# Two-bank row maxima on halves of the TensorE rows, in a transformer stack of two attentions and two feed-forwards

## The reference

```python
x = x + cross_attention(layernorm(x), ctx, mask, Wq, bq, Wk, bk, Wv, bv, Wo, bo)   # 16 heads of 16, 77 keys
x = x + mixture(layernorm(x), ...)            # 6 experts of 128, the top 2 of them weighted, gelu
x = x + shared_key_attention(layernorm(x), ctx, w_q, w_kv, w_concat)  # 16 query heads, one key/value head
x = x + fixed_point_ffn(layernorm(x), ...)    # 256 -> 1024 -> 256, rounded, piecewise-linear gelu
```

## Time and profile before

| | us |
|---|---|
| median of three runs | 789.1 (788.37 to 789.65) |
| the profiled execution's own time | 788.65 |
| its span | 786.4 |
| a block of the first attention (161.88 to 186.20 in the span) | 24.3 |
| a block of the second attention (498.33 to 518.90) | 20.6 |

### The profile page before, as it was taken

One profiled execution on the slowest core, in us unless ns is written; L12 is line 12 of the kernel. 1 busy time (PEld: TensorE's weight loads), 2 busy tenths in 40 slices (PEclk: granted clock), 3 DMA queues, 4 the chain that ended last, 5 costly groups with the idle time before them and its releaser, 6 DMA issues.

```text
span 786.4 us, 13553 instructions
## 1 busy us (share of the span) xinstructions
PE 730.7 (93%) x4372; PEld 548.4 (70%) x4372; DVE 645.4 (82%) x1546; ACT 513.6 (65%) x943; POOL 374.3 (48%) x323
## 2 busy tenths in 40 slices
PE   4799999999999999999998999999989999999995
PEld 3456666766558888888875555555558888888985
DVE  7658778777878878888887888998788999999995
ACT  3546556565654456555436777677778989989885
POOL 6374444334222223232214232222259999999884
PEclk9999999999999999999999999999999999999999
DMA  7975635564210000001047755755200000000001
GB/s 231 135 208 121 143 71 96 119 120 87 69 36 1 1 1 7 1 1 55 1 60 121 92 78 77 131 76 78 32 1 1 2 28 28 28 28 2 28 28 54
DMA packets 25101, 48.64 MB, mean 62 GB/s; under 512 B 3686, under 2 KB 7016, under 8 KB 24520
## 3 DMA queue, kind: packets, MB, share of 16 engines
q1 hardware_dynamic: 23366, 46.54, 30.6%
q10 hardware_dynamic: 1666, 1.24, 0.5%
HBM read 12.12 MB, written 4.19 MB: 21 GB/s over the span
## 4 chain that ended last, share of the span: by engine, by line
PE 53%; DVE 20%; issue 9%; ACT 7%; DMA 6%; POOL 4%; DVEq 0%; ACTq 0%; POOLq 0%
PE bank L141 15%; PE bank L649 7%; PE bank L413 6%; PE bank L436 6%; DMA qst<-mt 5%; PE bank L424 5%; PE bank L388 4%; DVE mx L342 4%; PE bank L416 3%; PE bank L812 3%; DVE fpart L768 3%; DVE x L617 2%; PE bank L391 2%; DVE fyl L780 2%; POOL fy L728 2%
## 5 line engine op out<-in xcount | busy, mean ns | idle before, releaser
L316 ACT ACTIVATE pt<-bank 77x512 f32<-77x512 f32 x256 | 141.0, 589 | 79.1 <-PE bank L416 59.3
L342 DVE TENSOR_REDUCE mx<-bank 128x4 f32<-128x308 f32 x256 | 108.6, 470 | 22.9 <-PE bank L391 12.3
L413 PE MATMUL bank<-qst,l_kst 128*77 128x512 f32 (+1 forms) x256 | 102.6, 416 | 16.8 <-DMA qst<-mt 10.5
L721 POOL TENSOR_TENSOR frise<-fg,fg 128x512 f32<-128x512 f32 x64 | 101.8, 1591 | 6.0 <-DVE fpart L768 0.8
L388 PE MATMUL bank<-l_kblk,qh 128*128 128x308 f32 x256 | 81.2, 339 | 7.6 <-DVE mx L342 6.4
L284 POOL TENSOR_TENSOR ol<-ot,oh 128x512 fp32r<-128x512 f32 x32 | 41.4, 1293 | 94.5 <-ACT oh L321 50.4
L103 POOL TENSOR_TENSOR rstd<-var,minus_half 128x4 f32<-128x4 f32 x32 | 34.8, 1088 | 102.5 <-DVE var L98 54.4
L617 DVE SCALAR_TENSOR_TENSOR x<-bank,eweight,x 128x256 f32<-128x256 f32 x192 | 79.5, 475 | 4.5 <-PE bank L649 4.2
L413 PEld LDWEIGHTS bank<-qst,l_kst 128*77 128x77 f32 (+1 forms) x256 | 36.5, 146 | 66.0 <-ACT pt L316 24.1
L114 ACT ACTIVATE xn<-x,shift,rstd 128x256 f32<-128x256 f32 (+1 forms) x128 | 67.0, 592 | 17.9 <-POOL shift L105 17.9
L812 PE MATMUL bank<-fw2h,fyh 128*128 128x256 f32 x256 | 73.3, 286 | 5.0 <-DVE fyl L780 4.7
(11 more groups left out here) (176 smaller groups left out, 2115.6 us busy)
## 6 DMA issues: line engine op xcount, KB each, us to landing
qst<-qh SPq DMA_DIRECT2D x64, 256.0 KB, 6.5
qst<-ql SPq DMA_DIRECT2D x32, 256.0 KB, 8.7
out<-x SPq DMA_DIRECT2D x8, 512.0 KB, 2.6
qst<-ml SPq DMA_DIRECT2D x8, 480.0 KB
x<-in_x SPq DMA_DIRECT2D x3, 1024.0 KB, 12.7
weights<-in_mlp_w SPq DMA_DIRECT2D x2, 1024.0 KB, 5.2
mraw<-in_mask SPq DMA_DIRECT2D x8, 154.0 KB
x<-in_x SPq DMA_DIRECT2D x2, 512.0 KB, 5.4
```

The lines of the kernel that those rows point to most:

```text
L316: self.nc.scalar.activation(self.pt[0:T, i // 4 % 2, i % 4, :], self.bank_of(G, i)[0:T, :], ACT.Exp).then_inc(self.probs, 1)
L342: self.nc.vector.reduce_max(out, banks[u % len(banks)][:, 0:4 * T].rearrange("q (p par t) -> q p par t", p=2, par=2), AX.X).then_inc(self. ...
L413: last = self.nc.tensor.matmul(out, layer.kst[rows, layer.stack(c * HC + 2 * k + par), b * T:(b + 1) * T], self.qst[rows, self.slot(G), c ...
L721: self.nc.gpsimd.tensor_tensor(self.rise[:, k % 2, :], self.g1[:, k % self.R, :], self.g0[:, k % self.R, :], ALU.subtract).then_inc(self.r ...
```

## The change

It does four things.

1. `max_unit` becomes `max_pair`. One pair takes the place of two units: 8 pairs in a block. A pair has two key matmuls, one with the rows 0 to 63 of `qh` and `kblk` into one bank, one with the rows 64 to 127 into the neighbouring bank, and then (first attention) two mask matmuls over all rows, one for each bank. The table `headsel` is changed so that heads 0 to 3 of a group have their rows in the lower half and heads 4 to 7 in the upper half. `take_maxima` takes one maximum over both banks: 616 elements to 8.
2. The two banks of `X` are one pair now, so every pair waits for the maxima of the pair before it (before: of the unit two before). The first blocks use two pairs in turn.
3. In the second attention, the two adds of the output to x become one over two banks (`add_both`), and so do the two low parts of the normed input (`rest_both`), which moves ahead of `fold`.
4. The orders by hand are changed: in the first attention, both query projections stand behind score 1, `weigh` of the block before behind score 3, the outputs behind score 11; in the second, the first half of the next block's queries stands ahead of score 0, and the second half behind score 1.

```diff
-    def max_unit(self, pe, layer, G, u, banks):
-        t, c, half = u // 4, u % 4 // 2, u % 2
+    def max_pair(self, pe, layer, G, v, banks):
+
+        t, c = divmod(v, C)
         pe.wait_ge(self.qh_ready, C * G + c + 1)
...
-        if u >= len(banks):
-            pe.wait_ge(self.max_taken, 16 * G + u - len(banks) + 1)
-        bank = banks[u % len(banks)][:, 0:4 * T]
-        tile = slice(t * P, (t + 1) * P)
-        keys = layer.kblk[:, c % layer.kc, self.batch(G), 4 * half:4 * half + 4, :]
-        last = self.nc.tensor.matmul(bank, self.qh[:, c, tile], keys, start=True, stop=not layer.masked)
+        if v >= len(banks):
+            pe.wait_ge(self.max_taken, 8 * G + v - len(banks) + 1)
+        pair = banks[v % len(banks)]
+        tile = slice(t * P, (t + 1) * P)
+        for par in range(2):
+            half = slice(64 * par, 64 * par + 64)
+            last = self.nc.tensor.matmul(pair[:, par, 0:4 * T], self.qh[half, c, tile],
+                                         layer.kblk[half, c % layer.kc, self.batch(G), 4 * par:4 * par + 4, :],
+                                         start=True, stop=not layer.masked)
         if layer.masked:
-            last = self.nc.tensor.matmul(bank, self.mh[:, tile], self.id5[:, 0:4 * T], start=False, stop=True)
+            for par in range(2):
+                last = self.nc.tensor.matmul(pair[:, par, 0:4 * T], self.mh[:, tile], self.id5[:, 0:4 * T], start=False, stop=True)
...
-            self.nc.vector.reduce_max(out, banks[u % len(banks)][:, 0:4 * T].rearrange("q (p par t) -> q p par t", p=2, par=2),
+            self.nc.vector.reduce_max(out, banks[v % len(banks)][:, :, 0:4 * T].rearrange("q par (p t) -> q par p t", t=T),
                                       AX.X).then_inc(self.max_taken, 1)
...
+    def rest_both(self, dve, n, banks, xh, xl):
+        dve.wait_ge(self.xh_ready, C * n + C)
+        self.nc.vector.tensor_tensor(xl[:, :, :], banks[:, :, :], xh[:, :, :].bitcast(F32), ALU.subtract).then_inc(self.xl_ready, C)
...
+    def add_both(self, dve, G):
+        dve.wait_ge(self.out_done, 2 * G + 2)
+        start = G % BLOCKS * NT
+        tiles = self.norm.x[:, start:start + NT, :].rearrange("p (k t) d -> p k (t d)", k=2)
+        self.nc.vector.tensor_tensor(tiles, tiles, self.WIDE[:, :, :], ALU.add).then_inc(self.added, 2)
...
+        PAIRS0 = {2: 0, 3: 1, 6: 2, 8: 4, 11: 5}
+        PAIRS1 = {1: 0, 4: 2, 6: 3, 7: 4, 10: 5, 11: 7}
...
-        "headsel": (2 * pair[:, None] + row[:, None] // DH == np.arange(HC)[None, :]).astype(np.float32),
+        "headsel": (row[:, None] // DH * PAIRS + pair[:, None] == np.arange(HC)[None, :]).astype(np.float32),
```

More of the change, by code:

```diff
@@ L846, in sem @@
             return stack.enter_context(nc.semaphore(n))
-        ps = [stack.enter_context(nc.psum_tensor(f"bank{i}", [P, N], F32)) for i in range(8)]
+        single = {i: stack.enter_context(nc.psum_tensor(f"bank{i}", [P, N], F32)) for i in (4, 5)}
+        double = {i: stack.enter_context(nc.psum_tensor(f"bank{i}{i + 1}", [P, 2, N], F32)) for i in (0, 2, 6)}
+        ps = [single[i][:, :] if i in single else double[i - i % 2][:, i % 2, :] for i in range(8)]
         x = place.at("x", m["x"], [P, BLOCKS * NT, D], F32)
@@ L1509, in _ @@
                 pe.wait_ge(id5_ready, 1)
[L1510 to L1512 removed]
+                for v in range(8):
+                    att.max_pair(pe, l0, 0, v, FIRST_MAX)
+                att.turn_maxima(pe, 0, ps[2])
                 pe.wait_ge(vo_in, 64)
```

205 lines of the change are left out of this document (103 added, 102 removed).

## The result

The changed kernel takes 815.5 us (median of 4 runs, 812.9 to 816.5) against 788.9 of the kernel before (4 runs): a ratio of 1.033, with a 95% interval of 1.031 to 1.036. The forecast was 797.5 us, with a range of 776 to 810. The direction was right and the size was not: 26.6 us instead of 8.6.

What follows compares the result with a forecast made beforehand. TensorE was taken to bound the first attention, TensorE and VectorE together the second. 788.65 + 9.9 (first attention) - 2 (second) + 0.5 (starts) = 797.05, plus 0.45 for the median: 797.5 us, range 776 to 810.

Steps and rivals of the forecast that it cites:

- stall at 173: First attention's block: TensorE loses 0.25 us waiting for VectorE near 173 us in the trace; spreading the pairs removes it.
- waits of 0.9 and 0.7: Second attention's block: TensorE waits 0.9 us for the maxima's DMA and 0.7 for VectorE's maxima; both were to go.
- 1.66 and 1.2 a block for half rows: TensorE's added time per block from half-row pairs: +1.66 us in the first attention, +1.2 in the second.
- 0.1 for the pair: Second attention's block: 0.1 us given back because pairs 2 and 4 have little work between them and the pair before.
- The form's price: TensorE's switch between all rows and half rows: 0.20 us each way; a first-attention pair takes 0.83 us against 0.572.
- no change of form: Rival: the half rows cost no change of the array's form, so the kernel gets faster, 768 us; 15%.
- not side by side: Rival: the two half-row matmuls don't run beside each other, 0.143 us more per pair, 812 us; 10%.
- The single pair of banks: Waits of each pair for one 0.79 us maximum: taken as covered, 0 in the first attention, 0.1 us in the second.
- the 2 us that the forecast named and did not take: First attention before the maxima's turn: if cover for the last maximum failed by 0.3 us a block, 2 us lost.
- This rival: Rival: VectorE, late by 0.4 us twice or more in each block, holds TensorE at the single pair, 804 us; 8%.
- The joins: Second attention: two-bank adds and low parts, with the two-bank maxima, make VectorE 0.8 us lighter per block.
- The starts: Maxima ahead of each attention's first block: 0 to 0.7 us in the first, -0.5 in the second; +0.5 taken together.

Runs made afterwards that it cites:

- two runs made for it: Kernel before with each unit's key matmul on half rows: 864.3 us; changed kernel with key, mask, key, mask order in the first attention: 855.4 us.
- banks by themselves: Changed kernel, half rows kept, but each bank of a pair waited for and taken on its own with single-bank maxima: 810.9 us; on full rows 786.3 us.
- the kernel with spread pairs: Changed kernel, half rows kept, with the pairs of each attention's first block spread over more scores: 813.1 us, ratio 1.029.
- the order stood alone: Changed kernel's new order with full rows, each bank waited for and taken on its own, and no joined adds or low parts: 781.9 us.

## Why the prediction was wrong

Its sum has the same parts as the table, so they can be set side by side (us; the forecast's from its own terms: stall at 173 and waits of 0.9 and 0.7 for the order, 1.66 and 1.2 a block for half rows, 0.1 for the pair):

```
                                         forecast   measured
order of the steps                          -13        -7.4
joined adds and low parts                     0        +4.4
single pair of banks, two-bank maximum       +0.7     +12.8
half rows, away from the starts             +20        +9.8
half rows at the starts                      +0.5      +6.6
sum                                          +8        +26.2
```

Measured are differences of the medians in the table above, so each is the cost of a part with those before it in place.

- **The form's price** (0.40 us in and out, 0.83 a pair, side by side): right, in the timeline and in two runs made for it. The first attention came to +1.6 us a block for +1.4; 1.5 of it are the half rows and 0.1 net the rest. The rivals "no change of form" and "not side by side" are both refuted by the two matmuls in one record of 0.41 us and the 0.34 us from there to the masks.
- **The single pair of banks**: this is the step that failed. "Does the single pair of banks make new waits there? ... I take 0", and 0.1 in the second attention. I compared the maximum's 0.79 us with what stands between two pairs and found it covered, but the cycle is longer than the maximum: both matmul streams, a hand-over, the maximum, a hand-over, 1.50 us. Two banks used in turn overlap one's filling with the other's taking (1.05 us for two units). Of the 12.8 us, 34 waits of 16.1 us in all instead of 13 of 5.0 are what TensorE's wait for both shows. In the first attention the cover did fail, by 0.3 us a block, the 2 us that the forecast named and did not take; in the second it was 0.5 us a block for 0.1. The forecast never looked at the first block of each attention, where no `weigh` and no output of a block before covers a pair: 4.5 us. This rival had 8% and 804 us; its mechanism was at work, with others on top.
- **The joins**: counted among what makes VectorE 0.8 us a block lighter, so that its waits go. The lightness is there (17.35 us busy for 19.00) and was worth less than nothing. The joined instruction waits for the later of its two sources, VectorE's queue stands behind it, and TensorE behind that: 0.26 us at the turned maxima, 0.44 at the query. The forecast added up VectorE's time and did not ask when each source is ready.
- **The starts**: "0 to 0.7". I priced a pair at the full clock and leaned on 4.25 us of idle time ahead of the first score. Nothing in the argument asked what the clock would do. With half rows it stood at 1.2 GHz for most of 20 to 50 us, pairs took 1.37 us instead of 0.83, and the cover ran out. The kernel with full rows at the starts alone is 6.6 us faster, 6.2 of it ahead of the first score in the profiles. But half rows alone don't bring the long low stretch about: with banks by themselves the same start was at the full level, and the kernel with spread pairs, the same up to the first score, had 10 us of it and its first score at 40.36. The same pairs also leave the clock at its full level in the steady blocks (1.00 in both windows above). So the cost is shown for the changed kernel, and its condition stays open.
- **The second attention's half rows** were too dear in the forecast, +1.2 us a block for 0.15 measured, since TensorE waits there for VectorE at the same places; with banks by themselves it is 0.6. This error hid a part of the others: that the block came to 20.8 us, near the 20.3 forecast, is luck.
- **The order**: right in kind, too large. Of the DMA wait and VectorE's waits (1.6 us a block in the second attention) 1.3 went when the order stood alone; in the first attention the spread-out pairs gave 0.2, as forecast. But the forecast counted seven such blocks in each attention, and the second attention's first block, which has no steps of a block before to move, became 1.4 us longer (19.5 to 20.9).

So the forecast had the new mechanism, the form's price, right and four of its five lines too cheap, by 28 us together; the fifth, half rows away from the starts, was 10 us too dear and hid a third of that.

## What to carry to other kernels

Before two instructions over one buffer each become one over both, write the cycle of that buffer down: fill, hand-over, take, hand-over. If the pair is the only one, the cycle is what must be covered, and the fixed cost saved (here 0.07 us of VectorE's time a round) is small beside what the cycle grows by where nothing covers it (1.50 us for 1.05). Over this kernel the producer's wait cost 8.1 us and the consumer's late start 4.7. A joined instruction also inherits the later of its waits: look at whether its sources come at the same time. And a cover of idle time is to be counted once, with the clock that the stretch will have.

## What the runs showed of the hardware

- Changing from 128 rows to 64 and back costs TensorE 0.38 to 0.40 us in all, with 128 columns of weights: 16 more pairs of changes in each block made it 5.8 us longer. The Trainium skill, page "TensorEngine Tiling (Array Packing)", Key Properties, says that a change of mode drains the engine; the runs agree that a change costs time, and add the size. Two half-row matmuls of 308 columns together save 0.13 us, so by these numbers (an estimate; no run has it) more than three pairs would have to stand behind one change in and out before they pay.
- VectorE reads two banks of PSUM in one instruction with no extra cost: 793 ns for 616 elements against 466 for 308, 1222 for an add of 1024 against 684 for 512.
- The granted clock is part of what a wait costs. In the changed kernel it fell at the end of the first attention's first block, at 65.3 us, behind the first of the two waits of 0.98 us shown above and within the second. It stood at 1.2 GHz for 54 us of the changed kernel and 18 of the one before; at half speed, 36 us more take at most 18 us of TensorE's work away, less where it stands waiting anyway. How much of each step of the table is this, and how much the wait itself, no run here separates.
